# A decoder layer on one core: the SBUF buffers of its three stages in another order of allocation

## What is computed

```python
x = x + mamba2(layernorm(x))                   # 64 heads of 64, state 128, inner width 4096
x = x + cross_attention(layernorm(x), ctx)     # 16 query heads, 4 key heads of 128, 64 context rows
x = x + moe(layernorm(x))                      # 8 experts, 2 per token, and 2 shared ones, width 640
```

## Time and profile before

| | |
|---|---|
| median of three runs | 1667.54 us |
| the profiled execution, its own time | 1666.68 us |
| span of its instructions | 1664.9 us |
| granted TensorE clock, mean | 0.989 |
| TensorE busy | 96% of the span, 9,876 matmuls |
| VectorE, ScalarE, GpSimd busy | 75%, 72%, 50% |
| DMA engines busy, queues q1 and q0 | 32.0% and 4.5% of 16 engines |

### The profile page before, as it was taken

The page is one execution under the profiler, slowest core; times in us unless marked ns, Lnnn a source line. Parts: engine busy times, 40 slices in busy tenths (PEclk is TensorE's granted clock), DMA queues, the critical chain, the costliest instruction groups (busy, mean ns, idle before and its releaser), DMA issues. The chain is left out here.

```text
span 1664.9 us, 29161 instructions
## 1 busy us (share of the span) xinstructions
PE 1592.1 (96%) x9876; PEld 1280.0 (77%) x9876; DVE 1250.4 (75%) x1954; ACT 1198.9 (72%) x2504; POOL 834.6 (50%) x677
## 2 busy tenths in 40 slices
PE   4998999999999999999999999999969999999999
PEld 3776777777777777777777667877748889999888
DVE  6899999999898999998899656766566534433355
ACT  5998899999999999999999566766624334444331
POOL 5798786565555555555565422211124563335460
PEclk8999999999999999999999999999979999999999
DMA  7555454444444454464542100000214323222231
GB/s 287 184 171 178 172 188 169 138 162 157 156 158 147 152 166 166 154 247 157 169 156 89 57 1 14 14 14 27 104 73 166 127 105 111 93 93 93 78 101 51
DMA packets 76238, 209.84 MB, mean 126 GB/s; under 512 B 9152, under 2 KB 32960, under 8 KB 74304
## 3 DMA queue, kind: packets, MB, share of 16 engines
q1 hardware_dynamic: 70432, 181.90, 32.0%
q0 software_dynamic: 5664, 26.09, 4.5%
HBM read 170.99 MB, written 36.96 MB: 125 GB/s over the span
## 5 line engine op out<-in xcount | busy, mean ns | idle before, releaser
L1011 PE MATMUL banks<-pair_hi,m_wxz 128*128 128x512 f32 x1024 | 352.3, 405 | 3.9 <-DVE pair_lo L664 2.3
L739 DVE SCALAR_TENSOR_TENSOR m_xc<-banks,m_cw,m_xc 128x510 f32<-128x510 f32 (+2 forms) x384 | 285.4, 743 | 11.0 <-ACT m_xc L502 1.3
L385 POOL TENSOR_TENSOR m_mat<-m_mat,m_cb_off 128x512 f32<-128x512 f32 x128 | 166.3, 1300 | 205.8 <-DVE m_mat L751 197.6
L516 ACT ACTIVATE m_mat<-m_a_all,m_cum 128x256 f32<-128x256 f32 x512 | 258.9, 506 | 1.6 <-PE m_ps_y L1052 1.6
L1068 PE MATMUL m_ps_out<-m_won,m_gT 128*128 128x256 f32 x1024 | 242.9, 380 | 4.7 <-POOL m_gT L394 3.2
L1011 PEld LDWEIGHTS banks<-pair_hi,m_wxz 128*128 128x128 f32 x1024 | 193.9, 189 | 42.8 <-issue 2.7
L394 POOL TENSOR_TENSOR m_gT<-m_gy,m_zs 128x512 f32<-128x512 f32 x128 | 167.0, 1305 | 107.2 <-DVE m_gy L781 106.9
L1068 PEld LDWEIGHTS m_ps_out<-m_won,m_gT 128*128 128x128 f32 x1024 | 191.4, 189 | 36.7 <-POOL m_gT L394 6.6
L519 ACT ACTIVATE m_mat<-m_a_all,m_cum 128x128 f32<-128x128 f32 x512 | 203.4, 397 | 0.0
L1011 PE MATMUL banks<-pair_lo,m_wxz 128*128 128x512 f32 x512 | 201.0, 393 | 0.0
L1052 PE MATMUL m_ps_y<-m_mat,m_xdt 128*64 128x256 f32 (+1 forms) x2048 | 194.7, 332 | 0.0
(11 more groups left out here) (348 smaller groups left out, 3400.4 us busy)
## 6 DMA issues: line engine op xcount, KB each, us to landing
m_a_all<-a_by_head SPq DMA_DIRECT2D x128, 512.0 KB, 4.0
m_wxz<-w_split SPq DMA_DIRECT2D x96, 512.0 KB, 5.0
w_split<-m_wxz SPq DMA_DIRECT2D x32, 512.0 KB, 3.0
raw<-in_w_gate_up POOLq DMA_DIRECT2D x9, 1280.0 KB, 6.8
raw<-in_w_xz SPq DMA_DIRECT2D x32, 256.0 KB, 3.9
raw<-in_w_down POOLq DMA_DIRECT2D x9, 640.0 KB, 7.8
x_sorted<-f_gT_hi SPq DMA_DIRECT2D x1, 4992.0 KB, 16.4
f_xg<-x_sorted SPq DMA_DIRECT2D x39, 128.0 KB, 2.6
```

Of the source, the lines that this page charges most:

```text
L385: pool.tensor_tensor(off, off, cb_off[:, g * BG:(g + 1) * BG, :].rearrange("p b t -> p (b t)").unsqueeze(1) .broadcast_to([P, HPT, BG * P] ...
L516: act.activation(first_rows(u, h, b), a_all[u][:, h, b * SEQ:(b + 1) * SEQ].rearrange("p (j t) -> p j t", t=P), ACT.Relu, bias=cum[:, t, h ...
L739: dve.scalar_tensor_tensor(out=out[:, :, k:], in0=ps[:, :, 0:SEQ - k], scalar=cw[:, c, TAPS - 1 - k:TAPS - k], in1=out[:, :, k:], op0=ALU. ...
L1011: last = pe.matmul(ps[:, :], w, a, start=m == 0, stop=m == len(terms) - 1)
```

## The change

The order of the `sb` calls changes in all three stages: those of the large buffers come first, those of the small ones behind them. Ahead of the large ones stand a few small ones whose sizes add up to a filling: in stage 1 `st` (384 bytes in each partition), in stage 2 `st`, `mv` and `neg_half` (640 bytes), in stage 3 `place` (128 bytes). No instruction, wait or transfer is added, removed or moved, and no buffer changes its size. Buffers that live through all stages stay where they are. The core of the diff:

```diff
@@ mamba_phase @@
-        cw = sb("cw", [P, conv_w.shape[1], TAPS])
+        st = sb("st", [P, NT, 6])
         won = sb("won", [P, NCT, HID])
-        ones = sb("ones", [P, 1])
         cb_diag = sb("cb_diag", [P, 2 * BG, 2 * P])
...
-        fold = sb("fold", [P, NH])
-        dtb = sb("dtb", [P, NH])
-        neg_a = sb("neg_a", [P, NH])
-        nw = sb("nw", [P, NCT])
         upto = sb("upto", [P, P])
...
-        st = sb("st", [P, NT, 6])
-        mv = sb("mv", [P, NT, 2])
-        rstd = sb("rstd", [P, NT])
...
         g_sum = sb("g_sum", [P, 2, TG])
+        cw = sb("cw", [P, conv_w.shape[1], TAPS])
+        fold = sb("fold", [P, NH])
...
@@ ffn_phase @@
-        st = sb("st", [P, LATE, 6])
...
         place = sb("place", [P, TOP, NT], U32)
-        table = sb("table", [P, 2 * TILES + E], I32)
...
         room = sb("room", [P, SLOTS * WIDE + 4 * I], F32R)
...
+        st = sb("st", [P, LATE, 6])
```

More of the change, by code:

```diff
@@ L134, in mamba_phase @@
         g_sum = sb("g_sum", [P, 2, TG])
+        cw = sb("cw", [P, conv_w.shape[1], TAPS])
+        fold = sb("fold", [P, NH])
+        dtb = sb("dtb", [P, NH])
+        neg_a = sb("neg_a", [P, NH])
+        nw = sb("nw", [P, NCT])
+        mv = sb("mv", [P, NT, 2])
+        rstd = sb("rstd", [P, NT])
         r_out = sb("r_out", [P, TPG])
+        ones = sb("ones", [P, 1])
         w_raw = raw[:, 0:RING * XZ].rearrange("p (r m) -> p r m", r=RING)
@@ L1210, in cross_attention_phase @@
         xT_lo = sb("xT_lo", [P, 2, KK, TT], F32R)
[L1211 to L1218, removed]
         x2_hi = sb("x2_hi", [P, KK, TT], F32R)
         x2_lo = sb("x2_lo", [P, KK, TT], F32R)
[L1221 to L1224, removed]
         qn_row = sb("qn", [P, D])
@@ L1227, in cross_attention_phase @@
         mask_sb = sb("mask", [P, TB, SE])
-        k_ss = sb("k_ss", [P, NP, NKV])
-        k_r = sb("k_r", [P, NP, NKV])
         kT = sb("kT", [P, NKV, NB * SE])
@@ L1238, in cross_attention_phase @@
         s = sb("s", [P, TB, NH, SE])
+        pT = sb("pT", [P, HP, P])
+        vw = sb("vw", [P, RING, HP, HID])
+        rstd = sb("rstd", [P, NT])
+        wr = sb("wr", [P, KK, E])
+        st2 = sb("st2", [P, TB, 6])
+        mv2 = sb("mv2", [P, TB, 2])
+        rstd2 = sb("rstd2", [P, TB])
+        bq_sb = sb("bq", [P, NH])
+        bv_sb = sb("bv", [P, NKV])
+        k_ss = sb("k_ss", [P, NP, NKV])
+        k_r = sb("k_r", [P, NP, NKV])
         s_max = sb("s_max", [P, NH])
         s_sum = sb("s_sum", [P, NH])
-        pT = sb("pT", [P, HP, P])
-        vw = sb("vw", [P, RING, HP, HID])
+        wo_raw = raw[:, 0:NH * HID].rearrange("p (h n) -> p h n", h=NH)
+        wq_hi, wq_lo = wq_parts
+        cT, wk_sb, wv_sb, bk_row = context_parts(xn_ffn)
+        wr_hi, wr_lo = wr_parts
+        kept = (NB - 2) * TT
+        x2_dram = nc.dram_tensor("x2_parts", [2, P, KK, kept], F32, kind="Internal").ap()
         earlier, first, both = routes
@@ L1940, in ffn_phase @@
         y_sorted = nc.dram_tensor("y_sorted", [TILES * P, HID], F32, kind="Internal").ap()
-        st = sb("st", [P, LATE, 6])
-        mv = sb("mv", [P, LATE, 2])
-        rstd = sb("rstd", [P, LATE])
-        neg_half = sb("neg_half", [P, LATE])
         xT_hi, xT_lo = xT_parts
         earlier, first, both = routes
[L1949 to L1954, removed]
         place = sb("place", [P, TOP, NT], U32)
-        table = sb("table", [P, 2 * TILES + E], I32)
-        weight = sb("weight", [P, TOP, NT])
-        total = sb("total", [P, NT])
         wgu_raw, wd_raw = expert_parts(raw, I)
@@ L1977, in ffn_phase @@
         gT_lo = sb("gT_lo", [P, 2, KK, P], F32R)
+        st = sb("st", [P, LATE, 6])
+        mv = sb("mv", [P, LATE, 2])
+        rstd = sb("rstd", [P, LATE])
+        neg_half = sb("neg_half", [P, LATE])
+        below = sb("below", [P, P])
+        counts = sb("counts", [P, 3, E])
+        steps = sb("steps", [P, NT])
+        tile_no = sb("tile_no", [P, TILES])
+        sign = sb("sign", [P, E])
+        ones = sb("ones", [P, P])
+        table = sb("table", [P, 2 * TILES + E], I32)
+        weight = sb("weight", [P, TOP, NT])
+        total = sb("total", [P, NT])
         zeros = gT_hi[:, 0].rearrange("p k t -> p (k t)").bitcast(F32)
```

## The result

The changed kernel takes 1670.63 us (median of 20 runs, 1668.72 to 1672.59), the kernel before 1666.99 us in as many runs beside it (1666.20 to 1668.38). The ratio is 1.0019 [1.0013, 1.0025]: 3.6 us slower, where 11 us less were forecast. The profiled execution took 1670.68 us with a span of 1668.9 us and a mean granted clock of 0.989; before it was 1666.68, 1664.9 and 0.989.

What follows compares the result with a forecast made beforehand. TensorE's matmul pace was taken as the bound: 1666.68 us less 11 us from stage 3, with 0 for stage 1, gives 1655.7, plus 0.9 for the median 1656.5 us. Own range 1652 to 1661.5; 8-in-10 range 1652 to 1671 us.

Steps and rivals of the forecast that it cites:

- What bounds the kernel: Whole kernel: TensorE, busy 96% of the span with small waits; new addresses change the time through the pace of its matmuls.
- the reading of the pace: Float32r matmuls: some 6 to 7 ns more each with the stationary operand 160 or 320 past a multiple of 512, not 256.
- 128 is as good as 256: Large buffers put at 128 past a multiple of 512 get the fast pace; weakly supported by L1832's 113 ns.
- 14.2 or 9.6 us in the sum, 11 taken: Stage 3, L2486, L2510, L2581 and L2561: 14.2 us gained with the fast pace throughout, 9.6 by the means; 11 taken.
- The price of L2486: Stage 3, 512 columns: 480 matmuls by 6.6 ns, 3.2 us gained.
- The terms of 256 columns: Stage 3, L2510 and L2581: 480 and 585 matmuls by 6.6 ns, gains of 3.2 and 3.9 us.
- The unknown cost: Stage 1, 1,536 matmuls of L1011 going from 256 to 128: 0 to 9 us lost, 0 taken.
- 256 is wanted: Rival: 128 is not enough, so stage 3 keeps its pace and L1011 loses 5 to 9 us; 1675 us, chance 0.16.
- the sign: Stage 1: L1011's low terms showing 399 ns for 393 would mean the prediction is wrong in the worse direction.
- What was costed at nothing: Plain float32 matmuls (L1807, L1785), VectorE's products, and the transfers of `wxz` and `a_all`: no cost either way.
- the case of no change: Rival: addresses don't set the pace; 1667.5 us, between 1664 and 1670.5, chance 0.22.
- the case of slower: Rival: 128 is not enough and stage 1's L1011 slows; 1675 us, between 1671 and 1678, chance 0.16.

Runs made afterwards that it cites:

- at512: Changed kernel with 384 bytes ahead of everything, so the large buffers of the stages start at multiples of 512 bytes; 1669.72 us, ratio to before 1.0006.
- b_e64: Changed kernel with gaps of 128 bytes in stages 1 and 3 and 64 in stage 2, `gT` moved by 64 bytes; 1665.39 us, ratio 0.9987.
- b_d64_at384: Changed kernel with gaps (128 bytes in stages 1 and 3, 64 in stage 2), `h` and `th` moved 64 inside `room`, 128 more ahead of everything; 1661.11 us.
- p64: Changed kernel with a gap of 64 bytes more ahead of the large buffers of each of the three stages; 1668.91 us, ratio 0.9999.

## Why the prediction was wrong

**What bounds the kernel: right.** The time moved with the sums of TensorE's starts (+4.0 us in the profiled executions, +3.6 us in the medians), and no other engine's busy time moved by more than 2 us.

**The step that failed is the reading of the pace.** The two paces were there, and addresses do set them; the cause was put on the wrong quantity. The prediction compared `wxz` with `wbc` under the same moving operand and concluded that the place of the stationary operand counts. But a comparison in which one of two addresses is held also changes their distance: 0 for `wxz`, +64 for `wbc`. Then it took 512 and 256 columns together. By distance these rows are 0 fast, +64 and -96 slow for 512 columns, and +64 fast, 0 slow for 256: two rules, where place gave one rule for all. The one rule was an accident of this layout. The rows of before could not tell the two readings apart, and the prediction named no rival by distance.

**"128 is as good as 256": no evidence.** L1832 moves 8 columns, and the prediction itself said that the weight load sets its pace; such a row says nothing of a stream of 256 or 512. Its median is 112 ns from start to start in all 15 kernels, with `x2` at 384 before, at 128 after and at 0 in at512.

**Stage 3: 14.2 or 9.6 us in the sum, 11 taken, about 1.6 measured.** L2486 gained 1.1 us (3.2 in the sum), of which 0.3 is pace, L2510 nothing (3.2), L2581 0.3 (3.9) and L2561 0.2 (3.9). `room` moved as a whole, so the distance inside it stayed 0, and that to `pair` went from -96 to -128. The price of L2486 was right and only its condition wrong: at distance 0 its pace is 227.1 ns for 233.2, which is 2.9 us for 480 matmuls. The terms of 256 columns were too big even at the best distance that was run: 1.2 us for L2510 (57.8) and 2.1 for L2581 (71.1). The 6.6 ns came from one undisturbed stretch; on average L2510 came at best to 117.5 ns, 2.5 under 120, and L2581 to 122.1 for 125.5. L2561 is at distance 0 in every kernel but b_e64, and its sum still lies between 138.9 and 139.8 us; its 3.9 us came nowhere, and what moves it is open.

**Stage 1: 0 taken out of 0 to 9, 3.7 us measured.** The unknown cost had the right lines and bounds, and the wrong end was taken. The rival "256 is wanted" forecast it in sign and place (L1011 at the pace of L983, which the timeline after shows), but its cause is out by at512 and b_d64_at384, and its price of 5 to 9 us was too high: L1011's mean between starts goes from 229.4 to 231.9 ns, 2.5 ns for 1,536 matmuls. Its low terms show 395 ns, between the 393 and 399 that were named as the sign.

**Stage 2 was missing.** The prediction saw that L1716's moving operand lay at 192 and used it only to say that the moving one doesn't matter. Its move to 128 cost 1.6 us.

**What was costed at nothing was nothing.** L1807 has 391 ns for 390, L1785 389 as before, VectorE's products 683 and 687 for 682 and 686 ns. `a_all` lands in 4.1 for 4.0 us and `wxz` in 4.9 for 5.0, and TensorE's wait for it is 1.6 us in both the earlier trace rows. By the Trainium skill, page "DMA: Bandwidth & Descriptors", section "How a descriptor splits into AXI transactions", a row of 4,096 bytes that starts at 128 takes 17 transactions and one that starts at 256 takes 16, an estimate of 0.3 us in the prediction. The landings differ by 0.1 us in opposite directions, so no run here shows a cost of it.

The range of 1652 to 1671 us held the time by luck: it reached that far up for the case of no change, while the case of slower, which came true in its sign, lay outside it. The sum was 14 us off. Of those, 9.4 us are gains of stage 3 that did not come, and 5.3 the losses of L1011 and L1716; what is left (L983 and L945, L1052 and smaller ones) comes to less than 1 us.

## What to carry to other kernels

To lay out buffers for TensorE, look at pairs: the two operands of each heavy matmul, and the difference of their addresses. Here 0 modulo 512 bytes was best for float32r matmuls of 512 columns and worst, with 128, for those of 256, which gained at 64; an alignment of every buffer to one multiple puts all pairs at one distance, and so can't serve both. When two rows are compared to find what an address does, list every quantity that differs between them, differences of addresses among them, and ask for a row in which they part before pricing a thousand matmuls by it.

## What the hardware showed that was not expected

- How far the weights lie from the moving operand sets the pace. 512 columns of float32r take 227 ns at distance 0, 229 to 232 at -64 and 232 to 234 ns at -128, -96, +64 and +128 (L983, L2486); 256 columns take 120 ns at 0, 118.5 at 32 and 117.5 to 118 ns at 64 either way and 96 (L2510). The Trainium skill's page "SBUF — State Buffer", section "Who interferes with whom", gives TensorE two read ports, independent of each other, and says that it never waits on anyone; b_d64_at384 and at512 speak against an independence down to the last percent. What makes the two meet, no run here shows.
- Plain float32 didn't care. L1785 has a median of 216 ns from start to start in all 15 kernels, with `vT` 32 bytes behind `raw` before and 0, 64, 128 or 192 ahead of it after, modulo 256. L1068 takes 216.0 to 216.5 ns; its operands stood at -32 before and at 0 in all others. L1807 shows nothing of it, since its two operands moved together.
- The same distance at the same places has more than one pace. L1716 at +64 has a median of 114 ns from start to start before, and of 117 to 118 ns in the eight other kernels with its operands at +64; in all of these but b_d64_at384 they lie at the very bytes of before. What decides it was not tried.
- The step of the first series from 0.43 to 0.23 us a matmul fell at 17.7 to 18.2 or at 20.1 to 21.0 us, whatever the layout. The granted clock of the stretch from 17.4 to 20.2 us reads 1.00 before and after, though the one has the fast pace there and the other the slow one. That reading is empty: the trace's record of the clock begins with a full clock at 17.6 us before and at 19.8 us after (17.6 to 18.2 us in five kernels, 18.9 to 20.8 in the other ten), and the view counts 1.00 where nothing is recorded. The slow pace of 0.43 us is that of p64 at 748 us, where 0.50 is recorded. So a pace says more of the clock at the start of a trace than the reading does.
